# A graph-network kernel on one Trainium2 core: GpSimd's row buffers are freed by VectorE's count of adds instead of TensorE's count of sums

## What is computed

```python
agg  = segment_sum(h[src], dst)                 # L0: linear + batch norm before, GELU after
agg  = segment_sum(xr[edge_type, src], dst)     # L1: three layers with 8 relations, ReLU
red  = segment_sum(h[src] + relvectors[rel], dst)      # L2: GRU cell on the result
out  = segment_sum(h[src] * alpha[..., None], dst)     # L3: attention with 4 heads
x    = layernorm(x + layer(x))                  # after each of the four
```

## Time and profile before

| | us |
|---|---|
| median of 3 runs | 9000.9 |
| lowest and highest run | 8998.14, 9028.72 |
| the profiled execution's own time | 8949.82 |
| its span, first to last instruction | 8947.9 |
| POOL busy / DVE busy / PE busy in the span | 5145.5 / 4792.8 / 6489.2 |

### The profile page before, as it was taken

The page is one execution under the profiler, slowest core; times in us unless marked ns, Lnnn a source line. Parts: engine busy times, 40 slices in busy tenths (PEclk is TensorE's granted clock), DMA queues, the critical chain, the costliest instruction groups (busy, mean ns, idle before and its releaser), DMA issues.

```text
span 8947.9 us, 105564 instructions
## 1 busy us (share of the span) xinstructions
PE 6489.2 (73%) x26061; PEld 4165.8 (47%) x26061; DVE 4792.8 (54%) x16511; ACT 2495.8 (28%) x7734; POOL 5145.5 (58%) x5401
## 2 busy tenths in 40 slices
PE   7886777779777787677776555556777776888881
PEld 4443555544345555344444333333444444656661
DVE  5665555455444444344443444444555556878888
ACT  3551111112111111011111222211222224666665
POOL 4555666640366665666665666656566555656550
PEclk9997777779899989788888776767889898999995
DMA  1003333334444445344446666673333345656662
GB/s 50 2 2 93 90 91 90 91 68 150 132 134 137 136 136 130 113 138 137 138 137 159 214 213 209 213 196 92 86 87 89 86 80 163 194 186 193 190 186 71
DMA packets 562316, 1141.95 MB, mean 128 GB/s; under 512 B 115031, under 2 KB 307516, under 8 KB 561598
## 3 DMA queue, kind: packets, MB, share of 16 engines
q0 software_dynamic: 252160, 659.72, 28.0%
q1 hardware_dynamic: 195886, 366.27, 11.8%
q10 hardware_dynamic: 113680, 109.21, 3.7%
HBM read 822.31 MB, written 312.46 MB: 127 GB/s over the span
## 4 chain that ended last, share of the span: by engine, by line
PE 39%; another core or an unknown queue 23%; issue 15%; DVE 15%; ACT 4%; DMA 1%; ACTq 1%; DVEq 1%; POOL 1%; SPq 0%; POOLq 0%
PE ps L1103 11%; PE ps L1319 5%; PE ps L1289 4%; PE ps L1507 3%; DVE AY L1773 3%; PE ps L1494 2%; PE ps L1451 2%; PE ps L1485 2%; PE ps L1480 1%; PE ps L1452 1%; PE ps L1092 1%; DVE oh L1756 1%; DVE rows L1756 1%; DVE edges L1635 1%
## 5 line engine op out<-in xcount | busy, mean ns | idle before, releaser
L1773 DVE TENSOR_TENSOR AY<-AY,ps 128x256 f32 (+1 forms) x4160 | 1740.6, 418 | 3160.2 <-remote 1678.5
L713 POOL DMA_INDIRECT g<-rel_d,edges x2496 | 2365.7, 948 | 1684.0 <-issue 666.9
L1103 PE MATMUL ps<-g,rows 128*128 128x256 f32 (+1 forms) x4160 | 1334.0, 442 | 262.5 <-issue 86.0
L1103 PE MATMUL ps<-g,oh 128*128 128x256 f32 (+1 forms) x4160 | 1394.0, 453 | 140.3 <-DVE oh L1756 53.0
L1103 PEld LDWEIGHTS ps<-g,rows 128*128 128x128 f32 x4160 | 846.5, 222 | 618.0 <-issue 366.2
L713 POOL DMA_INDIRECT g<-rows_d,edges x832 | 804.7, 967 | 536.8 <-issue 208.3
L1103 PEld LDWEIGHTS ps<-g,oh 128*128 128x128 f32 x4160 | 868.2, 227 | 410.0 <-issue 220.3
L713 POOL DMA_INDIRECT g<-in_x,edges x832 | 795.1, 956 | 444.7 <-issue 219.7
L1319 PE MATMUL ps<-AY,turned 128*128 128x512 f32 x1568 | 833.3, 659 | 179.9 <-issue 72.0
L2046 DVE TENSOR_REDUCE AY<-ps 128x4 f32<-128x512 f32 x832 | 570.8, 686 | 193.9 <-PE ps L1485 125.9
L740 ACT ACTIVATE wt<-ps 128x512 f32<-128x512 f32 (+1 forms) x448 | 250.0, 558 | 1464.0 <-remote 617.1
(11 more groups left out here) (384 smaller groups left out, 10040.4 us busy)
## 6 DMA issues: line engine op xcount, KB each, us to landing
rel_d<-wt ACTq DMA_DIRECT2D x392, 256.0 KB
turned_d<-AY SPq DMA_DIRECT2D x104, 512.0 KB
wt<-turned_d SPq DMA_DIRECT2D x104, 512.0 KB
AY<-marks_d SPq DMA_DIRECT2D x104, 512.0 KB
rel_d<-g SPq DMA_DIRECT2D x49, 1024.0 KB
g<-rel_d,edges POOLq DMA_INDIRECT x2496
marks_d<-oh SPq DMA_DIRECT2D x104, 256.0 KB
marks_d<-rows SPq DMA_DIRECT2D x104, 256.0 KB
```

Of the source, the lines that this page charges most:

```text
L713: pool.indirect_dma_start(out=g[:, j, 0:width], out_offset=None, in_=table, in_offset=bass.IndirectOffsetOnAxis(ap=edges[:, word, c:c + 1] ...
L1103: ins = pe.matmul(sum_slot(order, j), one_hot_at(j % OHS), g[:, j, 0:width], start=True, stop=True)
L1773: dve.tensor_tensor(tile_at(A, t, width), tile_at(A, t, width), sum_slot(order, j), ALU.add)\
```

## The change

In `gathers`, GpSimd waited before each even chunk c until TensorE had counted the pair of sums c-16, c-15. Now it waits until VectorE has counted the adds of that pair. `NCH * order + c + 2` is 17 plus the kernel's number of chunk c-15. The wait stands before the same gathers as before, and at none of the first sweep's first 16.

```diff
                 for c in range(NCH):
                     j = c % U
-                    if c % SUM_GROUP[order] == 0 and summed(order, c - U):
-                        pool.wait_ge(s_mm, summed(order, c - U))
+                    if c % 2 == 0 and NCH * order + c >= U:
+                        pool.wait_ge(s_add, NCH * order + c + 2)
                     pool.indirect_dma_start(
                         out=g[:, j, 0:width], out_offset=None, in_=table,
                         in_offset=bass.IndirectOffsetOnAxis(ap=edges[:, word, c:c + 1], axis=0)).then_inc(s_g[j], 16)
```

## The result

| | before | after |
|---|---|---|
| median of 4 runs each, same job (us) | 9006.68 (8998.14 to 9028.72) | 9231.72 (9220.47 to 9235.89) |
| the profiled execution (us) | 8949.82 | 9232.94 |
| granted TensorE clock in it | 0.839 | 0.832 |

After takes 1.0248 times as long as before, with a 95% interval of 1.0232 to 1.0264: 225 us more at the median. The forecast was 9006 us, within 8970 to 9050.

What follows compares the result with a forecast made beforehand. The prediction took TensorE, VectorE and ScalarE to set the pace, with GpSimd quicker and waiting. It added 4 us at sweep starts and ends and 1 us at the fourth sweep's end to 9000.9: 9006 us, range 8970 to 9050.

Steps and rivals of the forecast that it cites:

- What bounds the kernel: All sweeps: TensorE, VectorE and ScalarE set the pace, 1.48 us a chunk; GpSimd needs 1.25 us and waits for buffers.
- Step 1: Held gathers, read at one place in the second sweep: each starts 0.95 us later, 0.13 us behind the pair's second add.
- Step 2: Held gathers while the ring of 16 buffers is full: delays do not add up, a constant shift of about 1 us.
- Step 3: Middle of sweeps: only TensorE, waiting for later gathers, could feel the 0.95 us; taken as hidden, cost 0.
- The lead: Gathers running ahead of TensorE's sums: 13.7 us at one place, 10.7 us of it to spare, hiding the delay.
- Steps 4 and 5: Sweep starts and ends, 4 us; the fourth sweep's end, last six gathers some 15 us later, 1 us.
- The shared port: Gathers waking behind an add might meet VectorE's next one-hot, at most 0.28 us each; 1 in 100 to show.
- The rivals: Three other outcomes: slower at 9098 us, 11 in 100; faster at 8956 us, 7; change does nothing, 9001 us, 5.
- The first: Fourth sweep: GpSimd's lead is gone, so 102 waits of 0.95 us reach TensorE, 97 us, 9098 us; 11 in 100.
- wrong if a sweep in the middle grows by more than 15 us: Sign set beforehand for the middle sweeps: growth of one by more than 15 us would refute the forecast.
- waits past 150 us: Sign set beforehand: TensorE's waits for gathers, forecast under 90 us, would refute the forecast if past 150 us.

Runs made afterwards that it cites:

- r1: The changed kernel word for word, run in a job where the kernel before takes 7800 us: 7799.73 us, 0.9999 of before.
- x1: Kernel before without the gathers of odd chunks in sweeps two to four, nor the waits for them: 7672.64 us, 0.8528 of before.
- e4: Kernel before with GpSimd's wait on TensorE's count asking for two pairs of sums more, 12 buffers in effect: 8927.28 us, 0.9988 of before.
- x3: Kernel before, fetching only the first 64 of 256 floats of each row in sweeps two to four: 9008.44 us, 1.0001 of before.
- e5: Kernel before with GpSimd waiting for two pairs more of TensorE's sums, then for VectorE's adds: 7799.78 us, where before took 7800.3.

## Why the prediction was wrong

**What bounds the kernel: the step that failed.** "GpSimd is thus the quicker side by some 15%: it runs ahead until all 16 buffers are full, and then waits." The arithmetic was right (1.25 us for a gather, 1.48 us for a chunk), the reading was not. I took 1.48 us as the pace of the other engines, from which GpSimd's waits follow. In fact 1.48 us was GpSimd's own 1.25 us and its pauses: in the second sweep 1040 us and about 177 us, of which 148 are the 88 pauses of over 1 us. Without late counts the other engines do a chunk in 1.27 us or less (1060 / 832, r1), and with half the gathers in 1.04 us (863 / 832, x1, at a higher clock). They were waiting for counts, not working at their pace.

**Step 1, the delay of a held gather.** Right in kind, nearly in size. It forecast 0.13 us behind the second add's end; the trace after shows 0.27 us at the median, so the gather starts 1.27 us behind the first add's start and not 0.13: 1.14 us more, where I had 0.95. The reason that I gave there for the late count was wrong: "TensorE was streaming matmuls until 3017.12". At 3038.76 after, the count came while TensorE stood idle, between 3035.84 and 3042.20. I had seen the right fact, 5.0 us from the sum's end to both engines' start, and put an easy explanation on it instead of asking what else ended at that moment. GpSimd's last gather at 3013.88 stands in the earlier trace rows, 3.1 us ahead.

**Step 2, "does it add up? No, as long as the ring was full".** It did add up. The pauses went from a mean of 1.80, 1.68, 2.01, 2.14 and 1.83 us in the five sweeps to 2.47, 2.92, 2.76, 3.20 and 2.46, on 90, 88, 72, 66 and 135 of them before and 91, 68, 71, 62 and 101 after. In the second sweep that is 51 us more, and the sweep grew by 54. A shift is constant only if the next release does not depend on it. Here the release came about 3 us after the last gather of a run, so each pause began the next cycle later, by about half of the delay (225 of 448 us). The fifth sweep grew by 7 us with only 2 us more in its pauses, since it has fewer, longer ones; why it escaped I can't say.

**Step 3, who feels it.** TensorE's waits for gathers stayed at 20, as forecast, and that misled me. The engine behind did not miss the rows. It missed its counts. The lead played no part (e4).

**Steps 4 and 5.** Starts and ends are too small to be read. At the end of the fourth sweep the gather of chunk 830 starts at 6274.28, 0.27 us behind its pair's second add, but the six gathers before the last were not held by some 15 us: VectorE's wait for stored one-hots fell behind them this time. The sweep grew by 48 us like the others.

**The shared port.** I judged by the least and the median, 940 and 946 ns, which are the same after. They hide the tail. In the trace of before 196 of the 2699 gathers that a one-hot overlaps last over 1.0 us, the longest 1.27 us, against 6 of the 1461 others; in the trace after it is 130 of 2241 against 3 of 1919. The held gather at 3019.43 above, with 1.07 us, is one of them. "SBUF: two separate sides" in the Trainium skill's "SBUF — State Buffer" would have made gathers longer behind a VectorE instruction in a two-port mode. The tail goes that way, but no row tells the mode of a one-hot. It is no part of the loss: beyond 946 ns each, the overlapped gathers take 28 us in all five sweeps before and 17 us after.

**The rivals.** The first had the sign, and 11 in 100. Its price per pause was of the right kind (102 x 0.95 us in a sweep, where the fourth grew by 48 us), but its place and cause were not: it spoke of the fourth sweep alone and of a lead that is used up, to be seen as TensorE's waits for gathers, and those did not grow. The mark "wrong if a sweep in the middle grows by more than 15 us" caught the failure; "waits past 150 us" did not.

**What stays open.** Why TensorE's counts come late, and why they did so in four jobs and not in the other two, was not found. Shown is that the late pairs nearly went where half the gathers were left out, and stayed with a quarter of the bytes (x1, x3). That the release follows the last gather, and does not merely coincide with it, rests on the 3 us at the pauses, and half of the late pairs are let go outside pauses. No trace at 9000 us records when a gather landed, so the 0.7 us behind the landing in an expectation above is not shown. A matmul's end in a trace is worked out and not recorded, so a late count can't be told from a sum that itself ended late; the starts of the matmuls behind it run on. A gather spaced out on purpose, without being left out, was not tried. No version was found that beats before by more than 0.12% (e4, 0.9988, with an interval up to 1.0).

The traces hold one clue that no experiment followed. Those of the four jobs near 9000 us have 43,700 to 53,100 updates of semaphores each, and 1574 to 1723 for TensorE's count of sums, which is raised 2080 times. Those at 7800 us have 133,000 to 135,100, and 2080 or 2081. Either updates were merged on their way, which would fit counts that come several at once, or the profiler lost them. Most of what is missing comes from DMAs (26,600 to 34,700 against 107,000), and a gather adds 16 to its semaphore whatever its size.

## What to carry to other kernels

An engine whose waits are few long pauses between runs at its own cadence may be the bound. Cadence times count plus pauses gives the stage's length for any engine and proves nothing. Ask instead what ends each pause and what began just before it, whether the other engines were working or themselves waiting for a count, and move the release a little to see. Free a buffer by the earliest signal that allows it, since work put between a release and the next issue is paid on each pause, here by about half. And a delay is a constant shift only if the next release does not depend on it.

## What the runs showed of the hardware that was not expected

- The same program took 8935 to 9007 us in four jobs and 7800.3 us in two. In the traces of the faster ones 0 to 6 pairs in all five sweeps were late, the latest by 2.2 us (e5), and the granted clock was 0.913 (r1) instead of 0.839 (before). What the two kinds of job differ in is not known.
- In the trace of before adds started up to 20.2 us after the sum that they waited for, although VectorE had stood idle; TensorE was busy at some of these places and idle at others. Where a pause of GpSimd ended with them, that was 2.98 us after its last gather's start at the median; half of the late pairs came outside pauses.
- 416 gathers instead of 832 in the second sweep took the late pairs from 162 to 11 and the sweep from 1219 to 863 us; a quarter of the bytes gave nothing.
- Gathers that overlap a one-hot on VectorE last over 1.0 us in 196 of 2699 cases before, the others in 6 of 1461.
